# A feed-forward kernel's first product: high and low columns of h side by side, one matmul of 256 columns for two of 128

## The chip, the cores and the metric

The kernel runs on one core of a Trainium2 chip. The metric is device time in microseconds, from one launch. A profiled execution gives the trace: its span runs from the first to the last instruction, and the execution's own time is a little longer.

## The reference, cut to what matters

```python
x = x + gnn(layernorm(x), adj)            # two products with the normalised 2048 x 2048 adjacency
h = layernorm(layernorm(x)) * ln_gamma + ln_beta                   # 2048 tokens, 512 wide
sw1, sw2 = _bit_quant(shared_w1), _bit_quant(shared_w2)            # ternary times a scale per row
shared_out = silu(einsum('btd,fd->btf', h, sw1)) @ sw2.T           # f = 1024
probs = softmax(h @ router_w.T); top_prob, top_idx = max, argmax   # 8 experts
h1 = silu(einsum('btd,efd->ebtf', h, ew1)); eo = einsum('ebtf,edf->ebtd', h1, ew2)
x = x + shared_out + eo of the expert top_idx * top_prob
```

`_bit_quant` gives each row of a weight as -1, 0 or 1 times one scale, the mean of the row's absolute values. All is float32.

## The kernel before, in words

The first 410 us compute x1 (the graph part and its residual), turn the weights into ternary f16 matrices held in SBUF, and write h to memory, each row as a high f16 half and a low f16 half. The change doesn't touch that part, apart from names of PSUM banks.

Then come 39 tiles of 128 tokens: tiles 0 to 15 go through the shared expert, tiles 16 to 38 through one routed expert each, on rows gathered by token. Each has these steps:

- `first_product(n, u)` on TensorE: for 8 blocks `f` of 128 hidden units, 4 blocks `d` of the width and the two halves `h`, a matmul of 128 columns (L1517), all accumulated in float32 in PSUM. Weights are stationary, the columns of h (`ht`, loaded by a transposing DMA) move. High and low half of a block are added into the same 128 columns. The result takes two banks, and two tiles have a pair of banks each (`ps_h`).
- `tile` on VectorE, first part (L1234): for each half of 512 columns, `pre` = PSUM times `s1`, the scale of the weight's row, broadcast along the tokens.
- `tile` on ScalarE: for each half, Silu of `pre` into `h1` (L886) and a copy of `h1` times 16 as f16 (L893, the high half of h1).
- `tile` on VectorE, second part (L1244): for each half, h1 times 16 minus the high half, as f16 (the low half).
- `second_product(n, u)` on TensorE: 16 matmuls of 512 columns (L1545), for 8 blocks and two halves.
- `output` on VectorE (L1272, then L1275 in shared and L1277 in routed tiles): PSUM times the second weight's scale, added to the base row.

`pre` and `h1` are single buffers; h1's halves (`h1hl`) and the second product's banks (`ps_y`) are double. Every engine runs its own queue in order, written out by hand, with semaphores between them. TensorE's is first_product(n + 1), second_product(n), first_product(n + 2), and so on; for shared tiles the router's `logits` of some later tile stand between. VectorE's is, for tile n, the two scaled copies, work passed in as `between`, the two low halves, then output(n - 1), then `route`, the router's small steps. ScalarE's is, for tile n, Silu and high copy twice. In shared tiles two DMA issues stand behind them in ScalarE's queue: `next_base`, and `shared_store(n - 1)`, which waits for output(n - 1):

```python
                tile(n, r % 2, min(n, 2) if isinstance(n, int) else 2)
                if not (isinstance(n, int) and n < 2):
                    next_base(n, r % 2)
                if not (isinstance(n, int) and n == 0):
                    shared_store(n - 1, (r + 1) % 2)
```

Around tile 0 stand the last layer norms (`norm_parts`), a store of x1 (`store_x1`) and, after tile 1, four DMA issues for the column scales (`store_s2`, L849). Ahead of tile 12 ScalarE has an Exp for the router (L924), with a load of its table and one back for Silu; behind tile 12 it issues the store of the gates (`store_gate`, L901). Before routed tiles can be put out, their base rows are gathered on GpSimd's queue, after all shared tiles are stored (`y_stored`), and SyncE loads their scales (`load_scale`).

## Time and profile before

| | us |
|---|---|
| median of 3 runs | 705.63 |
| lowest and highest | 699.36, 707.70 |
| the profiled execution, its own time | 702.86 |
| its span | 701.2 |
| TensorE busy | 648.4 (92%) |
| VectorE busy | 469.2 (67%) |
| ScalarE busy | 389.6 (56%) |
| GpSimd busy | 151.7 (22%) |

Busy time counts instructions that compute; waits and the issuing of DMAs are not in it. The ends of matmuls in the trace are modelled, so the pace of a stream of them is read from start to start.

### The profile page before, as it was taken

Reading aid. Unit: us, or ns where it says so; the run is one execution under the profiler, and the core shown is the slowest. Engines: PE = TensorE matmul, PEld = TensorE weight load, DVE = VectorE, ACT = ScalarE, POOL = GpSimd, SP = SyncE. Lnnn points to the kernel's source line nnn. Section 1 sums busy time; section 2 is a strip of 40 time slices with the busy share of each in tenths; the row PEclk is TensorE's granted clock in tenths of the full one; section 3 lists DMA queues with packets and bytes.
Section 4 is the critical chain, followed back from the end, with each engine's and each line's share of the span. In section 5 each row is a group of like instructions: output and inputs, shape, how many; then the busy total and the mean of one; then the engine's idle time right before and its main releaser. Section 6 shows DMA issues by size and latency. Waiting matters only on the chain.

```text
span 701.2 us, 15954 instructions
## 1 busy us (share of the span) xinstructions
PE 648.4 (92%) x5281; PEld 381.6 (54%) x5281; DVE 469.2 (67%) x1031; ACT 389.6 (56%) x726; POOL 151.7 (22%) x171
## 2 busy tenths in 40 slices
PE   0798999999979999999998789999999999999995
PEld 0343444444434554445434367777767677777773
DVE  4878988566664555688788669756855565555553
ACT  1658648879986776777657653333432242424241
POOL 2234430000000000012323206200021353434322
PEclk9999999999999999999999999999999999999999
DMA  8999962675897777866576896643284876868641
GB/s 348 417 421 417 421 255 62 194 196 155 237 242 251 264 259 253 282 225 237 175 270 218 241 248 166 173 111 96 76 141 131 197 195 176 187 185 181 177 141 31
DMA packets 107103, 151.68 MB, mean 216 GB/s; under 512 B 64286, under 2 KB 64286, under 8 KB 102944
## 3 DMA queue, kind: packets, MB, share of 16 engines
q1 hardware_dynamic: 91280, 117.74, 53.5%
q0 software_dynamic: 6960, 20.99, 9.9%
q10 hardware_dynamic: 8800, 12.09, 5.7%
q8 instruction: 42, 0.69, 0.4%
q14 instruction: 21, 0.17, 0.1%
HBM read 119.57 MB, written 19.16 MB: 198 GB/s over the span
## 4 chain that ended last, share of the span: by engine, by line
PE 54%; DMA 14%; DVE 13%; ACT 9%; issue 7%; SPq 1%; POOL 1%; DVEq 0%; ACTq 0%; POOLq 0%
PE bank L1545 16%; PE bank L1517 16%; PE bank L1390 7%; PE bank L1392 7%; PE bank L1391 7%; DMA region<-in_adj_t 6%; ACT junk L748 4%; DMA work<-in_w 3%; ACT region L760 2%; DVE work L1096 2%; DVE region L986 2%; PE bank L1421 2%; DMA work<-in_adj_t 1%; DVE region L1192 1%; DVE region L982 1%
## 5 line engine op out<-in xcount | busy, mean ns | idle before, releaser
L1545 PE MATMUL bank<-region,work 128*128 (+1 forms) x624 | 141.6, 379 | 4.4 <-DVE work L1244 4.2
L886 ACT ACTIVATE work<-work 128x512 f32<-128x512 f32 x78 | 48.5, 622 | 171.1 <-DVE work L1234 171.1
L1390 PE MATMUL bank<-zreg,work 128*128 (+1 forms) x256 | 98.2, 384 | 12.3 <-DVE work L1164 10.9
L1517 PE MATMUL bank<-zreg,region 128*128 128x128 f16 x1728 | 100.9, 219 | 0.0
L1517 PEld LDWEIGHTS bank<-zreg,region 128*128 (+1 forms) x1728 | 98.1, 98 | 4.2
L1391 PE MATMUL bank<-zreg,work 128*128 (+1 forms) x256 | 98.2, 384 | 0.0
L1392 PE MATMUL bank<-zreg,work 128*128 (+1 forms) x256 | 98.0, 383 | 0.0
L1390 PE MATMUL bank<-region,work 128*128 128x512 f16 x192 | 74.1, 386 | 25.4 <-DVE region L1010 25.4
L1545 PEld LDWEIGHTS bank<-region,work 128*128 128x128 f16 x624 | 58.9, 98 | 70.4 <-issue 7.4
L748 ACT ACTIVATE junk<-work 128x512 f16<-128x512 f32 x124 | 77.6, 625 | 15.9 <-DMA work<-in_w 13.8
L1244 DVE SCALAR_TENSOR_TENSOR work<-work 128x512 f16<-128x512 f32 x78 | 53.7, 691 | 48.8 <-ACT work L893 48.8
L1234 DVE TENSOR_TENSOR work<-bank,s 128x512 f32<-128x512 f32 x78 | 50.2, 685 | 40.6 <-PE bank L1517 39.6
L1391 PE MATMUL bank<-region,work 128*128 128x512 f16 x192 | 74.2, 386 | 0.0
L1392 PE MATMUL bank<-region,work 128*128 128x512 f16 x192 | 74.2, 386 | 0.0
L760 ACT ACTIVATE region<-bank 128x1024 f16<-128x1024 int16 (+1 forms) x58 | 58.2, 1005 | 7.9 <-DVE region L1192 7.1
L1096 DVE TENSOR_SCALAR work<-work,thr 128x512 int16<-128x512 f32 (+1 forms) x96 | 57.7, 631 | 4.3
L804 ACT ACTIVATE work<-work 128x768 f16<-128x768 f32 (+1 forms) x48 | 36.8, 767 | 37.1 <-PE bank L1392 18.8
L591 POOL TENSOR_TENSOR rb<-rb,power 128x2 f32<-128x2 f32 x8 | 8.9, 1118 | 218.9 <-DVE rb L1145 218.9
L893 ACT ACTIVATE work<-work 128x512 f16<-128x512 f32 x78 | 49.1, 629 | 7.1
L1164 DVE SCALAR_TENSOR_TENSOR work<-work 128x768 f16<-128x768 f32 (+1 forms) x48 | 42.3, 884 | 10.4 <-ACT work L804 10.2
L1390 PEld LDWEIGHTS bank<-zreg,work 128*128 128x128 f16 x256 | 25.3, 99 | 41.2 <-DVE work L1164 12.9
L1390 PEld LDWEIGHTS bank<-region,work 128*128 128x128 f16 x192 | 19.1, 99 | 50.4 <-issue 20.7
(154 smaller groups left out, 946.8 us busy)
## 6 DMA issues: line engine op xcount, KB each, us to landing
work<-in_w SPq DMA_DIRECT2D x62, 512.0 KB, 4.1
region<-in_adj SPq DMA_DIRECT2D x16, 1024.0 KB, 10.7
region<-in_adj_t SPq DMA_DIRECT2D x16, 1024.0 KB, 7.5
work<-in_adj_t SPq DMA_DIRECT2D x32, 384.0 KB, 4.4
zreg<-s_scratch SPq DMA_DIRECT2D x24, 256.0 KB, 3.9
xb<-in_w SPq DMA_DIRECT2D x10, 512.0 KB, 4.2
zreg<-in_x SPq DMA_DIRECT2D x4, 1024.0 KB, 9.7
h_scratch<-hb POOLq DMA_DIRECT2D x16, 256.0 KB, 3.4
```

Source lines behind the costliest of these rows:

```text
L748: nc.scalar.activation(junk[:, :], src[:, a * D:(a + 1) * D], ACT.Abs, accum_out=asum[:, b, a:a + 1]).then_inc(abs_ok, 1)
L760: nc.scalar.activation(dst, pst16[turn_bank(q, b)], ACT.Sign).then_inc(wt_ok, 1)
L886: nc.scalar.activation(h1[:, cols], pre[:, cols], ACT.Silu).then_inc(h1_ok, 1)
L893: nc.scalar.activation(h1hl[:, b, 0, cols], h1[:, cols], ACT.Copy, scale=U_SCALE).then_inc(h1hi_ok, 1)
L1096: ins = nc.vector.tensor_scalar(words, rows, thr[:, b, 0, a:a + 1], None, ALU.mult)
L1234: nc.vector.tensor_tensor(pre[:, half * 512:(half + 1) * 512].rearrange("p (f t) -> p f t", f=4), ps_h[b][half][:, :].rearrange("p (f t) - ...
L1244: nc.vector.scalar_tensor_tensor(out=h1hl[:, b, 1, cols], in0=h1[:, cols], scalar=U_SCALE, in1=h1hl[:, b, 0, cols], op0=ALU.mult, op1=ALU. ...
L1390: nc.tensor.matmul(dst, a_hi, b_hi, start=start, stop=False, skip_group_check=True)
L1391: nc.tensor.matmul(dst, a_hi, b_lo, start=False, stop=False, skip_group_check=True)
L1392: return nc.tensor.matmul(dst, a_lo, b_hi, start=False, stop=False, skip_group_check=True)
L1517: last = nc.tensor.matmul(ps_h[b][f // 4][:, (f % 4) * P:(f % 4 + 1) * P], w, ht[n % RING][:, c:c + P], start=(f % 4 == 0 and d == 0 and h ...
L1545: last = nc.tensor.matmul(ps_y[b][:, :].rearrange("p (d c) -> p d c", d=DB), h1hl[:, b, h, f * P:(f + 1) * P], w, start=(f == 0 and h == 0 ...
```

## The change

One matmul of 256 columns takes a weight block over the high and the low columns, which lie side by side in `both` and in PSUM. A tile's first product then has 32 matmuls and fills four banks, 4 to 7, and there is one such buffer. ScalarE copies the low results into `pre` (two copies of 512 columns; the first waits for half of the product, `half_ok`), VectorE adds the high ones to them, and Silu applies the row scale by its per-partition `scale`, which needs an instruction for each of 8 blocks. For routed tiles VectorE first copies the 8 scales of the tile's expert to `s1_now`. The router's results move from banks 6 and 7 to 0 and 1, and the order of the first two tiles on TensorE changes with that.

```diff
--- before.py
+++ after.py
@@ -153,6 +153,7 @@
         thr = sb("thr", [P, 2, 2, 2], F32)
         s1 = sb("s1", [P, 2 * CHUNKS], F32)
         s2 = sb("s2", [P, CHUNKS], F32)
+        s1_now = dinv[:, :].rearrange("p (b f) -> p b f", b=2)
         rt = sb("rt", [P, DB, E], F32)
         r3 = sb("r3", [P, DB, 3, E], BF16)
 
@@ -200,18 +201,20 @@
         before = sb("before", [P, E, E], F32)
         unit = sb("unit", [1, TILES], I32)
 
-        bank = [ctx.enter_context(nc.psum_tensor(f"bank{i}", [P, 512], F32)) for i in range(8)]
-        acc = [bank[i][:, :] for i in range(8)]
-        pst = [bank[6][:, :].bitcast(F16), bank[7][:, :].bitcast(F16)]
-        pst16 = [bank[6][:, :].bitcast(I16), bank[7][:, :].bitcast(I16)]
-
-        ps_h = [[bank[4], bank[5]], [bank[0], bank[1]]]
+        bank = [ctx.enter_context(nc.psum_tensor(f"bank{i}", [P, 512], F32))[:, :] for i in range(4)]
+        banks47 = ctx.enter_context(nc.psum_tensor("banks47", [P, 2048], F32))
+        bank += [banks47[:, i * 512:(i + 1) * 512] for i in range(4)]
+        acc = list(bank)
+        pst = [bank[6].bitcast(F16), bank[7].bitcast(F16)]
+        pst16 = [bank[6].bitcast(I16), bank[7].bitcast(I16)]
+
+        ps_h = banks47[:, :].rearrange("p (f h t) -> p f h t", f=FB, h=2)
         ps_y = [bank[2], bank[3]]
-        ps_r = bank[7]
-        ps_lg = [bank[7], bank[6]]
+        ps_r = bank[0]
+        ps_lg = [bank[0], bank[1]]
         CNT0, LIST0 = 64, 256
-        ps_cnt = bank[7][:, CNT0:CNT0 + (NT + 1) * E].rearrange("p (t e) -> p t e", e=E)
-        ps_list = bank[7][:, LIST0:LIST0 + ROUTED_TILES]
+        ps_cnt = ps_r[:, CNT0:CNT0 + (NT + 1) * E].rearrange("p (t e) -> p t e", e=E)
+        ps_list = ps_r[:, LIST0:LIST0 + ROUTED_TILES]
 
 
         x_in = [sem("x_in0"), sem("x_in1")]
@@ -281,7 +284,10 @@
         base_got = [sem("base_got0"), sem("base_got1")]
         out_stored = [sem("out_stored0"), sem("out_stored1")]
         m1_ok = sem("m1_ok")
+        half_ok = sem("half_ok")
+        pre_lo = sem("pre_lo")
         pre_ok = sem("pre_ok")
+        s1_ok = sem("s1_ok")
         h1_ok = sem("h1_ok")
         h1hi_ok = sem("h1hi_ok")
         h1lo_ok = sem("h1lo_ok")
@@ -876,20 +882,33 @@
             store_x1(2, xg_z)
 
 
-            def tile(n, b, lead):
-
+            def tile(n, b, lead, shared=False):
+
+                for half in range(2):
+                    act.wait_ge(m1_ok if half else half_ok, n + 1)
+                    if lead >= 1:
+                        act.wait_ge(h1_ok, 8 * n - 4 + 4 * half)
+                    quarter = slice(4 * half, 4 * half + 4)
+                    nc.scalar.activation(pre[:, half * 512:half * 512 + 512].rearrange("p (f t) -> p f t", f=4),
+                                         ps_h[:, quarter, 1, :], ACT.Copy).then_inc(pre_lo, 1)
+                scales = s1[:, 0:FB] if shared else s1_now[:, b, :]
+                if not shared:
+                    act.wait_ge(s1_ok, n - NT + 1)
                 for half in range(2):
                     act.wait_ge(pre_ok, 2 * n + half + 1)
                     if lead >= 1:
                         act.wait_ge(h1lo_ok, 2 * n + half - 1)
                     cols = slice(half * 512, half * 512 + 512)
-                    nc.scalar.activation(h1[:, cols], pre[:, cols], ACT.Silu).then_inc(h1_ok, 1)
+                    for f in range(4 * half, 4 * half + 4):
+                        part_cols = slice(f * P, f * P + P)
+                        nc.scalar.activation(h1[:, part_cols], pre[:, part_cols], ACT.Silu,
+                                             scale=scales[:, f:f + 1]).then_inc(h1_ok, 1)
                     if lead >= 2:
                         act.wait_ge(m2_ok, n - 1)
                     if lead == 1:
                         act.wait_ge(ln_normed, 14)
                         act.wait_ge(x1_stored, 16 * NT // 2)
-                    act.wait_ge(h1_ok, 2 * n + half + 1)
+                    act.wait_ge(h1_ok, 8 * n + 4 * half + 4)
                     nc.scalar.activation(h1hl[:, b, 0, cols], h1[:, cols], ACT.Copy, scale=U_SCALE).then_inc(h1hi_ok, 1)
 
             def shared_store(n, b):
@@ -908,7 +927,7 @@
 
             def shared_tile(n, r):
 
-                tile(n, r % 2, min(n, 2) if isinstance(n, int) else 2)
+                tile(n, r % 2, min(n, 2) if isinstance(n, int) else 2, True)
                 if not (isinstance(n, int) and n < 2):
                     next_base(n, r % 2)
                 if not (isinstance(n, int) and n == 0):
@@ -1227,15 +1246,14 @@
 
             def tile(n, b, shared, lead, u, between=()):
 
+                if not shared:
+                    dve.wait_ge(h1_ok, 8 * n - 8)
+                    nc.vector.tensor_copy(s1_now[:, b, :], s1[:, ds(u * FB, FB)]).then_inc(s1_ok, 1)
                 for half in range(2):
-                    dve.wait_ge(m1_ok, n + 1)
-                    if lead >= 1:
-                        dve.wait_ge(h1_ok, 2 * n + half - 1)
-                    nc.vector.tensor_tensor(
-                        pre[:, half * 512:(half + 1) * 512].rearrange("p (f t) -> p f t", f=4),
-                        ps_h[b][half][:, :].rearrange("p (f t) -> p f t", f=4),
-                        s1[:, ds(u * FB + half * 4, 4)].rearrange("p (f a) -> p f a", a=1).to_broadcast([P, 4, P]),
-                        ALU.mult).then_inc(pre_ok, 1)
+                    dve.wait_ge(pre_lo, 2 * n + half + 1)
+                    cols = slice(half * 512, half * 512 + 512)
+                    rows = pre[:, cols].rearrange("p (f t) -> p f t", f=4)
+                    nc.vector.tensor_tensor(rows, ps_h[:, 4 * half:4 * half + 4, 0, :], rows, ALU.add).then_inc(pre_ok, 1)
                 for work_, *args in between:
                     work_(*args)
                 for half in range(2):
@@ -1269,7 +1287,7 @@
                     if lead >= 2:
                         dve.wait_ge(out_stored[b], slot_count(n - NT, b))
                 scale, scaled = (s2bc[:, 1, :], o_t[:, b, :]) if shared else (s2bc[:, b, :], s2bc[:, b, :])
-                chained(nc.vector.scalar_tensor_tensor(out=scaled, in0=ps_y[b][:, :], scalar=1.0 / U_SCALE, in1=scale,
+                chained(nc.vector.scalar_tensor_tensor(out=scaled, in0=ps_y[b], scalar=1.0 / U_SCALE, in1=scale,
                                                        op0=ALU.mult, op1=ALU.mult), y_seq, n + 1)
                 if shared:
                     nc.vector.tensor_tensor(base_t[:, b, 0:D], base_t[:, b, 0:D], scaled, ALU.add).then_inc(y_ok, 1)
@@ -1505,18 +1523,17 @@
 
             def first_product(n, u):
 
-                b = n % 2
                 columns_in(n)
-                if n >= 2:
-                    pe.wait_ge(pre_ok, 2 * n - 2)
+                if n:
+                    pe.wait_ge(pre_ok, 2 * n)
+                both = ht[n % RING].rearrange("p (h d t) -> p d h t", h=2, d=DB)
                 for f in range(FB):
                     for d in range(DB):
                         w = w1t[:, ds(u * (4 * CHUNK) + (f // 2) * CHUNK + d * 2 * P + (f % 2) * P, P)]
-                        for h in range(2):
-                            c = (h * DB + d) * P
-                            last = nc.tensor.matmul(ps_h[b][f // 4][:, (f % 4) * P:(f % 4 + 1) * P], w,
-                                                    ht[n % RING][:, c:c + P], start=(f % 4 == 0 and d == 0 and h == 0),
-                                                    stop=False, skip_group_check=True)
+                        last = nc.tensor.matmul(ps_h[:, f, :, :], w, both[:, d, :, :], start=(f % 2 == 0 and d == 0),
+                                                stop=False, skip_group_check=True)
+                    if f == FB // 2 - 1:
+                        last.then_inc(half_ok, 1)
                 last.then_inc(m1_ok, 1)
 
             def logits(n):
@@ -1542,7 +1559,7 @@
                         nxt = load_unit(ahead)
                     w = w2t[:, ds(u * (4 * CHUNK), 4 * CHUNK)].rearrange("p (d f c) -> p f d c", d=DB, f=FB)[:, f, :, :]
                     for h in range(2):
-                        last = nc.tensor.matmul(ps_y[b][:, :].rearrange("p (d c) -> p d c", d=DB),
+                        last = nc.tensor.matmul(ps_y[b].rearrange("p (d c) -> p d c", d=DB),
                                                 h1hl[:, b, h, f * P:(f + 1) * P], w,
                                                 start=(f == 0 and h == 0), stop=False, skip_group_check=True)
                 last.then_inc(m2_ok, 1)
@@ -1553,14 +1570,13 @@
 
 
             pe.wait_ge(x1_ok, Y_GROUPS[2][0])
-            pe.wait_ge(wt_ok, SHARED_CHUNKS)
+            pe.wait_ge(wt_ok, 2 * CHUNKS)
             first_product(0, 0)
             pe.wait_ge(r3_ok, 1)
-            pe.wait_ge(wt_ok, 2 * CHUNKS)
+            pe.wait_ge(x1_ok, NT - 2)
             logits(0)
-            pe.wait_ge(x1_ok, NT - 2)
+            logits(1)
             first_product(1, 0)
-            logits(1)
             pe.wait_ge(x1_ok, NT)
             second_product(0, 0)
             logits(2)
```

## Rows read from the trace of the kernel before

**Rows 1.** Stretches: each engine's busy us and instructions, clock, DMA share, GB/s.

```profile
424.00:489.00 65.00, 65.00 (x813) 47.99 (x811) 47.08 (x104) 22.76 (x38) 14.11 (x17) 1.00 0.47 130
...
560.00:683.00 123.00, 123.00 (x1381) 88.90 (x1379) 71.24 (x107) 43.36 (x72) 50.73 (x51) 1.00 0.69 178
```

**Rows 2.** Timeline, TensorE, from 566 us: start, us, line, operation, count.

```profile
566.85 3.62 PE L1545 MATMUL bank<-region,work 128*128 x16
570.30 3.74 PE L1517 MATMUL bank<-work,region 128*128 128x128 f16 x64
573.87 3.62 PE L1545 MATMUL bank<-region,work 128*128 x16
```

**Rows 3.** Timeline, VectorE, tile 20.

```profile
560.13 0.75 DVE L1277 SCALAR_TENSOR_TENSOR zreg<-zreg 128x512 f32<-128x512 f32 x1
561.18 1.29 DVE L1234 TENSOR_TENSOR work<-bank,s 128x512 f32<-128x512 f32 x2 [0.29 <-issue]
...
564.61 0.69 DVE L1244 SCALAR_TENSOR_TENSOR work<-work 128x512 f16<-128x512 f32 x1 [0.55 <-ACT work L893]
...
565.94 0.75 DVE L1277 SCALAR_TENSOR_TENSOR zreg<-zreg 128x512 f32<-128x512 f32 x1
```

**Rows 4.** Timeline, ScalarE, tile 20.

```profile
561.99 0.63 ACT L886 ACTIVATE work<-work 128x512 f32<-128x512 f32 x1 [3.21 <-DVE work L1234]
562.71 0.63 ACT L893 ACTIVATE work<-work 128x512 f16<-128x512 f32 x1
563.24 0.61 ACT L886 ACTIVATE work<-work 128x512 f32<-128x512 f32 x1
563.95 0.63 ACT L893 ACTIVATE work<-work 128x512 f16<-128x512 f32 x1
```

**Rows 5.** Groups of ScalarE by shape: busy us, mean ns, then idle.

```profile
L737 ACT ACTIVATE zreg<-bank,dinvz 128x512 f16<-128x512 f32 x16 | 9.8, 689 | 3.1 <-PE bank L1392 3.1
L699 ACT ACTIVATE junk<-zreg,mv 128x512 f16<-128x512 f32 x12 | 8.7, 722 | 1.6 <-DVE mv L961 1.3
...
L924 ACT ACTIVATE zreg<-zreg 128x128 f32<-128x128 f32 x1 | 0.3, 310 | 0.0
```

**Rows 6.** Timeline, VectorE, output in a shared tile.

```profile
447.49 0.69 DVE L1275 TENSOR_TENSOR zreg<-zreg 128x512 f32<-128x512 f32 x1
```

**Rows 7.** Timeline, ScalarE (ACTq: its queue's DMA issues), shared tiles.

```profile
448.35 0.36 ACTq L897 DMA_DIRECT2D base_scratch<-zreg  x1
...
493.40 0.63 ACT L886 ACTIVATE work<-work 128x512 f32<-128x512 f32 x1 [4.64 <-DVE work L1234]
...
498.21 0.36 ACTq L897 DMA_DIRECT2D base_scratch<-zreg  x1
498.74 1.28 ACT L924 ACT_TABLE_LOAD   x1 [2.74 <-DVE zreg L1275]
...
506.58 0.35 ACTq L897 DMA_DIRECT2D base_scratch<-zreg  x1
508.10 0.40 ACTq L901 DMA_DIRECT2D base_scratch<-zreg  x1
...
535.44 0.35 ACTq L897 DMA_DIRECT2D base_scratch<-zreg  x1
```

**Rows 8.** Timeline, ScalarE, DMA issues ahead of tiles 0 and 2.

```profile
414.55 0.38 ACTq L841 DMA_DIRECT2D x_scratch<-work  x1
...
428.40 1.43 ACTq L849 DMA_DIRECT2D s_scratch<-s2t  x4
```

**Rows 9.** Timeline, VectorE, low halves of tile 0, start of tile 1.

```profile
417.89 1.28 DVE L1244 SCALAR_TENSOR_TENSOR work<-work 128x512 f16<-128x512 f32 x2
...
421.83 1.28 DVE L1234 TENSOR_TENSOR work<-bank,s 128x512 f32<-128x512 f32 x2
```

**Rows 10.** Timeline, VectorE, output of tile 17.

```profile
553.18 0.69 DVE L1272 SCALAR_TENSOR_TENSOR zreg<-bank,zreg 128x512 f32<-128x512 f32 x1 [4.78 <-DMA zreg<-s_scratch]
```

**Rows 11.** Timeline, TensorE, the last second product.

```profile
690.79 3.62 PE L1545 MATMUL bank<-region,work 128*128 x16 [0.87 <-DVE work L1244]
```

## The prediction

> **What bounds the kernel now.** I read the stretches table first. From 560 to 683 us, which is routed tiles only, TensorE is busy all of the 123 us, VectorE 71 and ScalarE 43 [rows 1]; the shared tiles of 424 to 489 us look the same. The timeline of TensorE shows what fills it: 64 narrow matmuls of the first product, 3.57 us from their start to the next group's, then 16 wide ones of the second, 3.45 us to the next [rows 2]. A tile costs 7.02 us, and nothing stands between the groups.
>
> So the other two engines have slack, but busy time doesn't say how much, because they hand work to each other and each works its queue in order. I followed tile 20 through both. VectorE starts the scaled copy out of PSUM at 561.18, ScalarE its Silu 0.81 later, then come the high copy (+0.72), the second Silu (+0.53), the second high copy (+0.71), VectorE's second low half (+0.66), the second operation of the output (+1.33), and from that one's start it is 1.05 until VectorE can start the next tile (560.13 to 561.18) [rows 3, 4]. The sum is 0.81 + 0.72 + 0.53 + 0.71 + 0.66 + 1.33 + 1.05 = 5.81 us. It is a ring: VectorE cannot take the next tile's first operation before the output, which stands behind the low halves, which wait for ScalarE. Today the ring takes 5.81 us and TensorE 7.02, so 1.2 us of slack hide it. Whatever the change adds to the ring beyond 1.2 us is paid in every tile.
>
> **The first product.** Columns streamed stay 8192 a tile. A matmul of 128 columns takes 3.57 / 64 = 55.8 ns, of 512 columns 3.45 / 16 = 215.6 ns [rows 2]: a line through both gives 109.1 ns for 256, 3.49 us for 32, and TensorE's tile 6.94. The gain is at most 0.08 x 39 tiles = 3 us, and nothing where TensorE isn't the bound.
>
> The halves now fill banks 4 to 7, so there is one buffer: first_product(n+1) waits for tile n's last add. A second product of 3.45 us lies between, and the add is done about 0.6 (copy) + 0.7 (add) + 0.6 us of queueing and handing over after the first product ends. This wait costs nothing, except in tile 1, where a longer term covers it.
>
> **Silu.** Two instructions of 512 columns become eight of 128 with a per-partition scale. The trace has no such one. Nearest are an Exp of 128 columns, 0.31 us, and a 512-column one with a per-partition operand, 0.72 against 0.63 without [rows 4, 5]. So one takes 0.31 + 0.09 = 0.40 us. Successive independent ones overlap by 0.10 (the high copy from 562.71 runs to 563.34, the Silu behind it starts at 563.24 [rows 4]), so they start 0.31 apart. Four and the handing over to the high copy: 3 x 0.31 + 0.40 + 0.09 = 1.42 us, where it is 0.72 and 0.71 now. That adds 1.41 us to the ring. Bounds: below, if the operand cost nothing and 0.22 lay between starts, 3 x 0.22 + 0.31 + 0.09 = 1.06, 0.7 a tile less; above, no overlap at all, 3 x 0.40 + 0.40 + 0.09 = 1.69, 0.54 more. I take the middle, as both rows measure their part.
>
> The Trainium skill (ScalarE: Activation LUTs, What ACT_TABLE_LOAD costs) gives 186 ns + 0.833 ns per element, 93 ns for each pointer operand and 93 ns overlap. By these figures the starts are 0.29 apart and four take 1.36 us; the sum below would be about 5 us less. The Trainium skill (VectorE: DVE Perf Modes, The TRN2 errata) speaks against the edit: a fixed latency is paid for each instruction, so many small tiles pay it again and again. The trace agrees: an eighth of a tile costs 0.31 us and half a tile 0.63.
>
> **The ring of the routed tiles.** VectorE's add takes the place of its multiply (same elements, one PSUM source; VectorE's operations of this size take 0.69 to 0.75 [rows 3], I take 0.69). ScalarE's two copies of the low halves come before it in another idle time: the first waits for half of the first product, done long before VectorE is through with the output. The copy of the scale and its two waits add some 0.2 us in front of the add (0 to 0.4). The ring is 5.81 + 1.41 + 0.20 = 7.42, and 7.45 with something for the loop's branch. It exceeds TensorE's 6.94, so it becomes the bound, by 0.43 us over today's 7.02.
>
> **The ring of the shared tiles** is worse. There ScalarE's queue has, behind each tile's high copies, the store of the tile before, which waits for VectorE's output. Today what follows the store is a Silu with time to spare. After the change the first low copy of the next tile stands there, and VectorE can't add without it. Within a tile, from the first Silu: 1.42 + 0.53 + 1.42 + 0.66 = 4.03 to the second low half, 1.33 + 0.69 to the end of the output [rows 3, 6]: 6.05. The store is issued 0.17 later (448.18 to 448.35), takes 0.36, and the next ScalarE instruction comes 0.17 behind it (498.57 to 498.74): 0.70 [rows 6, 7]. The copy from PSUM, by the one that has a per-partition operand, takes 0.69 - 0.09 = 0.60 [rows 5], handing over 0.03, the add to the Silu 0.81. Period: 6.05 + 0.70 + 0.60 + 0.03 + 0.81 = 8.19 us, against 7.02 now and the logits' short matmuls. Bounds without those of the Silus: 8.0, if the issue hides 0.2, to 8.4.
>
> **The sum**, as times of each tile's first Silu.
> Tile 0: the x1 store goes out at 414.55 [rows 8] and takes 0.38, the copy follows at 415.10, first Silu 416.54. Waiting for all transposes before tile 0's first product costs nothing: it still ends before that copy's turn. Tile 0's low halves end at 421.26, and 2.66 us of layer-norm work stand ahead of the next tile, as now (419.17 to 421.83 [rows 9]): tile 1 at 424.73. Then the output, the store, four DMA issues of the column scales (1.43 [rows 8]) and the copy, all in a row now: tile 2 at 434.40. Tile 3, 0.4 late through layer-norm work ahead of the low halves: 442.99. Eight periods of 8.19: tile 11 at 508.5. It is at 493.40 now [rows 7]: +15.1.
> Tile 12: 6.05 + 0.70, table load 1.28 and Exp 0.31 [rows 5, 7], two copies 1.0, table load for Silu and handing over 1.3 = 10.65. Tile 13: the store of the gate goes out 1.52 after the tile's own, takes 0.40 [rows 7], and stands ahead of the copy: 6.05 + 0.17 + 1.52 + 0.40 + 0.17 + 1.44 = 9.75. Tiles 14 to 16, three periods: 24.6. Tile 16 at 553.5.
> From the end of tile 15's output to that of tile 17 runs a chain of DMAs (store, gathers, transposes, scales): 535.27 to 553.18, 17.9 us [rows 7, 10]. VectorE stalled 4.8 us for it, most of it inside its slack. After the change it ends at 559.55 + 17.9 = 577.5, where the two tiles would be ready at 573.8. The stall is 3.7, all of it on the path. Tile 19 at 580.7, tile 20 at 588.1, against 561.99 [rows 4]: +26.1, so +11.0 between tiles 11 and 20.
> Eighteen routed periods, 134.1, and 4.8 from the last first Silu to the last second product: 138.9. It was 690.79 - 561.99 = 128.8 [rows 4, 11]: +10.1. What follows is unchanged.
> Total +15.1 + 11.0 + 10.1 = +36.2 us on the profiled execution's 702.86: **739 us**. That execution is 0.4% below the median 705.63, so the ratio to the median is 1.047.
>
> **The rivals.**
> A. TensorE stays the bound, and the kernel ends faster than before: the narrow Silus and copies fit into slack, 0.08 us is won in each tile, the bigger matmuls pay: 702.86 - 3 = 700. It decides if both rings stay under 6.94, that is, 0.5 us less than I have in the routed and 1.25 in the shared tiles. For it: ScalarE is busy only 43 of 123 us. Against it: the ring, which can be read off. 7%.
> Its stronger form is that the weight loads of the narrow matmuls, not their columns, set their pace. With half the loads the first product would then come down to the second's pace for a column, 8192 x 215.6 / 512 = 3.45 us, 4.7 us in all: 698. The two rows speak against it, 0.436 ns a column in the one and 0.421 in the other [rows 2]. 1%. The Trainium skill (TensorE: Matmul & The Clock Gate, Back-to-back issue gap) has such a rule, about 81 ns for a matmul of 128 columns in a stream with weight loads and 131 for 512; the trace's 55.8 and 215.6 agree with neither.
> B. Four narrow Silus cost about as much as one wide one (0.81 with its scale). The rings are then some 6.2 and 7.0, only the start, tiles 12 and 13 and the longer end cost something: about 710. For it: they are independent and queued. Against it: the 0.31 us of the Exp, which is mostly fixed cost. 9%.
> C. They don't overlap, as each reads a per-partition operand: 0.54 x 38 tiles more, 760. For it: no row has two such back to back that weren't held up otherwise. 12%.
> My forecast, both rings bound, has the rest, 70%.
>
> **Range and chances.** The bounds of the copy of the scale, the DMA issue and the Silus' spacing move the forecast by 0.5 us a tile either way, 19 us: 720 to 758. With C it holds 8 in 10: 720 to 760. Within 2% of 705.6 (about what a measurement of this kernel can tell from no change) are A and B, up to 719.7: 0.16; faster by over 2% (below 691.5) is none of the cases: 0.01; slower 0.83.
>
> **What the profile after would show.** TensorE idle before the second product in nearly all tiles, released by VectorE's low half (L1244 now); its share down from 92% to about 88%. Silus of 0.40 us starting 0.31 apart. First Silus 8.2 us apart in shared tiles and 7.45 in routed ones. VectorE idle before its add in shared tiles, released by ScalarE's low copy, which starts 0.7 us behind the output's end. The first product 3.49 us. Wrong would be: no idle time ahead of the second product (A), Silus closer than 0.2 (B) or 0.4 apart (C), or a low copy that starts ahead of the store's wait, which would bring the shared tiles down to the routed ones' pace.

## The result and the profile after

| us | before | after |
|---|---|---|
| median of 4 executions (lowest to highest), same chip | 703.68 (699.36 to 707.7) | 728.12 (727.63 to 728.99) |
| ratio, 95% interval | | 1.0358 (1.032 to 1.0396) |
| the profiled execution | 702.86 | 728.99 |
| its span | 701.2 | 727.4 |

The change makes the kernel 24 us slower. The prediction was 739, with 720 to 760 as its range. It started from a median of 705.63; a fourth execution of the kernel before, 701.74, lowers that to 703.68. The first part of the page after:

```profile
PE 659.1 (91%) x4033; PEld 364.4 (50%) x4033; DVE 473.3 (65%) x1054; ACT 483.6 (66%) x1038; POOL 155.4 (21%) x171
```

ScalarE works 94 us more (483.6 for 389.6), and no engine has over 91% of the span. As in the prediction, the busy shares don't say who sets the time. The stretches table after has the same columns as [rows 1]:

```profile
424.00:489.00 65.00, 58.35 (x464) 39.17 (x463) 41.06 (x91) 36.22 (x92) 14.79 (x17) 1.00 0.44 117
...
560.00:683.00 123.00, 119.79 (x798) 77.20 (x796) 69.24 (x116) 80.31 (x200) 54.56 (x52) 0.99 0.73 176
```

TensorE, busy without a break in both stretches before, now idles 6.65 us of 65 in the shared tiles, and 3.2 of 123 in the routed ones.

Where the 26.2 us of span came from can be read off the timeline of ScalarE, by the start of each tile's first high copy (L893 before, L912 after):

| first high copy of tile | 0 | 3 | 11 | 12 | 13 | 19 | 20 | 38 | end of span |
|---|---|---|---|---|---|---|---|---|---|
| before | 415.81 | 438.35 | 494.12 | 502.63 | 510.18 | 556.90 | 562.71 | 688.05 | 701.2 |
| after | 416.20 | 442.94 | 507.75 | 518.22 | 527.57 | 578.48 | 585.49 | 713.54 | 727.4 |
| later by | 0.4 | 4.6 | 13.6 | 15.6 | 17.4 | 21.6 | 22.8 | 25.5 | 26.2 |

Half is gone by tile 11: shared tiles 3 to 11 are 8.10 us apart where they were 6.97 (two short gaps of a tile catching up among them; at even pace, from tile 6 on, they were 7.1 to 7.2 apart). Tiles 12 to 20 add 9.2 more. The 18 routed periods from tile 20 to 38 are 7.11 apart where they were 6.96, 2.7 us in all.

The timeline of ScalarE after, first in a shared and then in a routed tile:

```profile
455.86 0.36 ACTq L916 DMA_DIRECT2D base_scratch<-zreg  x1
456.41 1.08 ACT L892 ACTIVATE work<-banks 128x512 f32<-128x512 f32 x2 [2.77 <-DVE zreg L1293]
457.84 1.28 ACT L904 ACTIVATE work<-work,s 128x128 f32<-128x128 f32 x4 [0.35 <-DVE work L1256]
459.15 0.63 ACT L912 ACTIVATE work<-work 128x512 f16<-128x512 f32 x1
...
598.48 1.28 ACT L904 ACTIVATE work<-work,dinv 128x128 f32<-128x128 f32 x4 [0.50 <-DVE work L1256]
599.78 0.63 ACT L912 ACTIVATE work<-work 128x512 f16<-128x512 f32 x1
600.32 1.26 ACT L904 ACTIVATE work<-work,dinv 128x128 f32<-128x128 f32 x4
...
602.65 0.60 ACT L892 ACTIVATE work<-banks 128x512 f32<-128x512 f32 x1 [0.41 <-PE banks L1533]
```

The shared tile shows the longer ring that the prediction describes: ScalarE idles 2.77 us because the store's issue waits for VectorE's output, and the low copies stand behind it. In the routed tile no store is in the way. Compare with [rows 4]: a Silu's start to its high copy's was 0.72 us and is 1.30. VectorE's timeline after, from the end of that shared ring and from two routed tiles:

```profile
455.00 0.69 DVE L1293 TENSOR_TENSOR zreg<-zreg 128x512 f32<-128x512 f32 x1
...
457.04 1.29 DVE L1256 TENSOR_TENSOR work<-banks,work 128x512 f32<-128x512 f32 x2 [0.79 <-ACT work L892]
...
596.60 0.75 DVE L1295 SCALAR_TENSOR_TENSOR zreg<-zreg 128x512 f32<-128x512 f32 x1
597.55 0.17 DVE L1251 COPY dinv<-s 128x8 f32 x1 [0.19 <-issue]
597.67 1.29 DVE L1256 TENSOR_TENSOR work<-banks,work 128x512 f32<-128x512 f32 x2
600.45 0.69 DVE L1262 SCALAR_TENSOR_TENSOR work<-work 128x512 f16<-128x512 f32 x1 [1.49 <-ACT work L912]
602.28 0.69 DVE L1262 SCALAR_TENSOR_TENSOR work<-work 128x512 f16<-128x512 f32 x1 [1.14 <-ACT work L912]
...
603.61 0.75 DVE L1295 SCALAR_TENSOR_TENSOR zreg<-zreg 128x512 f32<-128x512 f32 x1
604.84 0.17 DVE L1251 COPY dinv<-s 128x8 f32 x1 [0.48 <-issue]
```

From the output's last operation to the next tile's copy of the scales it is 0.95 us in the one tile (596.60 to 597.55) and 1.23 in the next (603.61 to 604.84). The second one crosses the end of the loop's body, which holds two tiles. So routed tiles alternate between 7.01 and 7.28 us, and the mean of the two, 7.145, is what the ring costs.

TensorE's timeline after, behind the stall of tile 19 and later in the routed tiles:

```profile
577.91 5.54 PE L1533 MATMUL banks<-zreg,region 128*128 128x256 f16 x32 [2.71 <-DVE work L1256]
583.28 3.62 PE L1562 MATMUL bank<-region,work 128*128 x16
...
593.68 3.66 PE L1533 MATMUL banks<-work,region 128*128 128x256 f16 x32
597.17 3.62 PE L1562 MATMUL bank<-region,work 128*128 x16
600.63 3.66 PE L1533 MATMUL banks<-work,region 128*128 128x256 f16 x32
...
635.61 3.86 PE L1533 MATMUL banks<-work,region 128*128 128x256 f16 x32
639.42 3.71 PE L1562 MATMUL bank<-region,work 128*128 x16
```

From 593.68 to 600.63 a tile costs TensorE 6.95 us, 3.49 for the first product and 3.46 for the second. There it is behind the ring and catching up at 0.2 us a tile. By 635.61 it has caught up: the first product then takes 3.81 us (to 639.42), and no idle time stands before either group. The program has no wait inside a first product. What has become late is TensorE's queue, which hands the matmuls to the engine: it passes the wait ahead of this product (L1528) at 634.85, just behind VectorE's second add (it ends at 634.81), only 0.76 us before the first matmul. For every weight block the queue forms an address in a register (`FUSED_REGOPS`), most of them 124 ns apart:

```profile
L1533 PEldq FUSED_REGOPS  x31: 46/46/46, 635.1 to 639.1; - x31
```

The first 22 matmuls start 109 ns apart; then the queue's lead is used up and the others start 124 ns apart, once 182. A group whose queue is late looks busy in this view, so the distance from start to start must be read, not the idle column.

### The profile page after: what moved, and what is told of

The parts are those of the page before. It is cut to its first block, busy times and chain, and to the rows that moved or that the text cites. A ratio compares the mean times of both kernels' runs of the same rounds, so it can differ in the third digit from the quotient of the medians.

```text
span 727.4 us, 13812 instructions
## 1 busy us (share of the span) xinstructions
PE 659.1 (91%) x4033; PEld 364.4 (50%) x4033; DVE 473.3 (65%) x1054; ACT 483.6 (66%) x1038; POOL 155.4 (21%) x171
## 4 chain that ended last, share of the span: by engine, by line
PE 42%; DVE 16%; ACT 14%; DMA 13%; issue 9%; ACTq 2%; SPq 1%; POOL 1%; DVEq 0%; POOLq 0%
PE banks L1533 10%; PE bank L1562 9%; DMA region<-in_adj_t 6%; ACT work L904 6%; PE bank L1408 5%; PE bank L1410 5%; PE bank L1409 5%; DMA work<-in_w 5%; ACT junk L754 3%; PE banks L1410 2%; PE banks L1409 2%; PE banks L1408 2%; DVE region L1005 2%; DVE zreg L1290 2%; DVE work L1115 2%
## 5 line engine op out<-in xcount | busy, mean ns | idle before, releaser
L1262 DVE SCALAR_TENSOR_TENSOR work<-work 128x512 f16<-128x512 f32 x78 | 54.0, 693 | 93.0 <-ACT work L912 92.9
L1533 PE MATMUL banks<-zreg,region 128*128 128x256 f16 x864 | 104.1, 279 | 10.4 <-DVE work L1256 9.1
L1533 PEld LDWEIGHTS banks<-zreg,region 128*128 (+1 forms) x864 | 85.2, 99 | 29.5 <-issue 11.4
L892 ACT ACTIVATE work<-banks 128x512 f32<-128x512 f32 x78 | 44.7, 592 | 72.5 <-DVE zreg L1293 34.9
L754 ACT ACTIVATE junk<-work 128x512 f16<-128x512 f32 x124 | 77.6, 626 | 17.4 <-DMA work<-in_w 15.1
L1408 PE MATMUL bank<-zreg,work 128*128 128x512 f16 (+1 forms) x192 | 73.8, 384 | 11.5 <-DVE work L1183 10.5
L904 ACT ACTIVATE work<-work,dinv 128x128 f32<-128x128 f32 x184 | 58.4, 388 | 28.3 <-DVE work L1256 27.5
L1410 PE MATMUL bank<-zreg,work 128*128 128x512 f16 (+1 forms) x192 | 73.5, 383 | 0.0
L1409 PE MATMUL bank<-zreg,work 128*128 128x512 f16 (+1 forms) x192 | 73.5, 383 | 0.0
L1408 PE MATMUL bank<-region,work 128*128 128x512 f16 x112 | 43.7, 390 | 25.4 <-DVE region L1029 25.4
L766 ACT ACTIVATE region<-banks 128x1024 f16<-128x1024 int16 (+1 forms) x58 | 58.2, 1006 | 8.2 <-DVE region L1211 6.8
L1256 DVE TENSOR_TENSOR work<-banks,work 128x512 f32<-128x512 f32 x78 | 50.5, 686 | 15.3 <-ACT work L892 15.3
L912 ACT ACTIVATE work<-work 128x512 f16<-128x512 f32 x78 | 49.1, 630 | 3.5
L1533 PE MATMUL banks<-work,region 128*128 128x256 f16 x384 | 45.1, 274 | 2.4 <-DVE work L1256 2.4
L904 ACT ACTIVATE work<-work,s 128x128 f32<-128x128 f32 x128 | 40.6, 388 | 6.7 <-DVE work L1256 6.6
L1409 PE MATMUL bank<-region,work 128*128 128x512 f16 x112 | 43.9, 392 | 0.0
```

The lines of the kernel that those rows point to most:

```text
L754: nc.scalar.activation(junk[:, :], src[:, a * D:(a + 1) * D], ACT.Abs, accum_out=asum[:, b, a:a + 1]).then_inc(abs_ok, 1)
L766: nc.scalar.activation(dst, pst16[turn_bank(q, b)], ACT.Sign).then_inc(wt_ok, 1)
L904: nc.scalar.activation(h1[:, part_cols], pre[:, part_cols], ACT.Silu, scale=scales[:, f:f + 1]).then_inc(h1_ok, 1)
L912: nc.scalar.activation(h1hl[:, b, 0, cols], h1[:, cols], ACT.Copy, scale=U_SCALE).then_inc(h1hi_ok, 1)
L1256: nc.vector.tensor_tensor(rows, ps_h[:, 4 * half:4 * half + 4, 0, :], rows, ALU.add).then_inc(pre_ok, 1)
L1262: nc.vector.scalar_tensor_tensor(out=h1hl[:, b, 1, cols], in0=h1[:, cols], scalar=U_SCALE, in1=h1hl[:, b, 0, cols], op0=ALU.mult, op1=ALU. ...
```

## The experiments

A ratio is to the kernel before on the same chip. "Pace" is the distance between first high copies of successive tiles.

**e1: the store behind the next tile's low copies.** In the kernel after, shared_store(n - 1) is issued between the low copies and the first Silu of tile n + 1, no longer ahead of the copies (the gate's store moves with it; the base load stays).

```diff
+            for issue, *args in late:
+                issue(*args)
...
-                if not (isinstance(n, int) and n == 0):
-                    shared_store(n - 1, (r + 1) % 2)
+                late = [(shared_store, n - 2, r % 2)]
```

> The changed kernel with the shared tiles' stores (and the gate's) issued by ScalarE behind the next tile's two low copies instead of ahead of them. My theory (a ring of VectorE and ScalarE, in which the store's wait and issue delay the low copy): first Silus of shared tiles come 7.2 us apart instead of 8.1, as TensorE with its logits then binds; tiles 3 to 11 give back 7.4 us, tiles 13 to 17 some 3 more; total 728.1 - 11 = 717. The routed tiles stay at 7.14. Rival, that the narrow Silus alone make ScalarE's chain too long: the pace stays near 8.1 and the total at 726 to 728.

Measured: 716.25 us (715.7 to 719.93), ratio 1.0228 (1.0189 to 1.0267), span 713.9. ScalarE's timeline in shared tiles:

```profile
455.66 0.60 ACT L892 ACTIVATE work<-banks 128x512 f32<-128x512 f32 x1 [0.41 <-PE banks L1533]
456.58 0.36 ACTq L918 DMA_DIRECT2D base_scratch<-zreg  x1
457.74 1.28 ACT L906 ACTIVATE work<-work,s 128x128 f32<-128x128 f32 x4 [1.49 <-DVE work L1256]
```

The low copies now wait for TensorE and not for VectorE's output, and the store lies in idle time. Tile 3 to 11 takes 58.88 us where it took 64.81, a pace of 7.36 for 8.10 (7.2 was expected); routed tiles stay at 7.01 and 7.28. The position of one DMA issue in ScalarE's queue is worth 9 us by the ratios (1.0358 less 1.0228, of 703), and 11.4 by the spans from tile 0 on (13.4 less the 2.0 by which tile 0 was earlier): some 40% of the loss. This confirms the second ring of the prediction.

**e2: one Silu of 512 columns for four of 128.** In the kernel after, with the row's scale left out, so the scale is not applied. All else, copies and single buffer included, stays.

```diff
-                    for f in range(4 * half, 4 * half + 4):
-                        part_cols = slice(f * P, f * P + P)
-                        nc.scalar.activation(h1[:, part_cols], pre[:, part_cols], ACT.Silu,
-                                             scale=scales[:, f:f + 1]).then_inc(h1_ok, 1)
+                    nc.scalar.activation(h1[:, cols], pre[:, cols], ACT.Silu).then_inc(h1_ok, 4)
```

> The changed kernel with one Silu of 512 columns per half, without the per-row scale (the scale of the first weight is left out of the result). My theory: the chain from Silu to high copy falls from 1.31 to 0.72 us, twice in a ring. Routed ring 7.14 - 1.18 = 5.96, shared 8.10 - 1.18 = 6.92, both under TensorE's 6.95 and 7.15: total 708 to 711, the rest over 703.7 being start, tiles 12 and 13 and the end. Rival, that the single buffer in PSUM or the low copies hold TensorE up: over 720.

Measured: 707.17, ratio 1.0075 (1.0053 to 1.0098), span 703.3. That is just under the expected 708 to 711. Routed tiles run at 6.95 us, TensorE's own pace. Shared tiles 3 to 11 are 6.90 apart: there VectorE and ScalarE catch up with TensorE, whose own groups are 7.15 apart (466.09 to 473.24). So the many short Silus are necessary for nearly all of the loss: without them about 5 us of 25 remain (by the ratios), and these lie ahead of tile 3 (26.17 us from tile 0 to tile 3, against 22.54 before and 26.74 after) and at tile 12 (9.78 against 8.51).

**e3: TensorE's part alone.** The 32 matmuls of 256 columns and the single buffer, in the kernel before; VectorE scales the high half as before, and the low half's sum is never read, so it is left out of the result.

```diff
+                        last = nc.tensor.matmul(ps_h[:, f, :, :], w, both[:, d, :, :], start=(f % 2 == 0 and d == 0),
+                                                stop=False, skip_group_check=True)
...
-                        ps_h[b][half][:, :].rearrange("p (f t) -> p f t", f=4),
+                        ps_h[:, 4 * half:4 * half + 4, 0, :],
```

> TensorE's part alone: 32 matmuls of 256 columns into the one buffer of four banks, but the other engines work as before the change (VectorE scales the high half, one Silu per half); the low half of h is computed and left out. My theory: TensorE binds, first product 3.49 us, 0.08 us less in each of 39 tiles, 703.7 - 3 = 700.5; the single buffer costs nothing. Rival, that the wait for the one buffer costs: first products start late, over 706.

Measured: 703.55 over 10 runs (701.95 to 706.68), ratio 1.0012 (0.9987 to 1.0037), span 700.5. The 3 us did not show. TensorE's gain is there where TensorE is the bound: routed tiles are 6.95 us apart, not 7.02, and tile 21 to 38 takes 117.96 us for 119.24. It is given back in two places, first at tile 12 (gap 9.77 for 8.51). ScalarE's and TensorE's timelines there:

```profile
498.96 0.31 ACT L930 ACTIVATE zreg<-zreg 128x128 f32<-128x128 f32 x1
500.87 1.28 ACT L892 ACT_TABLE_LOAD   x1 [1.60 <-issue]
```

```profile
502.40 3.66 PE L1521 MATMUL banks<-zreg,region 128*128 128x256 f16 x32
507.89 1.17 PE L1597 MATMUL bank<-zreg 128*128 128x23 f16 x16 [1.84 <-DVE zreg L1352]
```

Here Silu's table is loaded 1.60 us after the Exp ends; in the kernel before it begins at once (Exp at 500.03, load at 500.36). TensorE then idles 1.84 us. The other place is behind tile 19's stall, where tile 20 to 21 takes 7.14 us for 6.10; with two buffers TensorE could have a first product ready ahead, with one it can't, which is argued and not shown. The load of the table begins 0.07 us behind the end of VectorE's first multiply for tile 12 (500.11 + 0.69 = 500.80), for which that Silu waits; in the kernel before it begins ahead of the multiply (501.18). So here it stands behind the Silu's wait, and its 1.28 us lie on the path. e2 has the same (add ends at 503.72, load at 503.79), which is part of its loss at tile 12. What puts the load behind the wait was not tried.

**e4: eight Silus of 128 columns in the kernel before**, with a per-partition scale of one, VectorE's multiply and both buffers kept. It leaves nothing out.

```diff
-                    nc.scalar.activation(h1[:, cols], pre[:, cols], ACT.Silu).then_inc(h1_ok, 1)
+                    for f in range(4 * half, 4 * half + 4):
+                        part_cols = slice(f * P, f * P + P)
+                        nc.scalar.activation(h1[:, part_cols], pre[:, part_cols], ACT.Silu,
+                                             scale=before[:, 1, 0:1]).then_inc(h1_ok, 1)
```

> The kernel before with eight Silus of 128 columns and a per-partition scale of one; everything else as before. My theory: the ring grows from 5.81 by 1.18 to 6.99 us, and by another 0.28 over a loop's back edge, so 7.13 on average in routed tiles against TensorE's 7.02: 2 us there, 1 in the start, 1 at tile 12, 0.6 at the end, total 708. Rival, that ScalarE's added work is hidden wherever TensorE binds: 704 or less. Rival, that narrow Silus alone explain most of the change's loss: over 716.

Measured: 721.88 (716.95 to 724.46), ratio 1.0295 (1.0267 to 1.0324), span 715.3. It missed: the Silus alone bring most of the loss, some 20 us, where 708 was expected. Routed tiles alternate between 6.97 and 7.26, as worked out. But shared tiles 3 to 11 run at 7.41, because there the router's small steps on VectorE stand in the ring, which the expectation left out: 0.85 us to the next multiply (463.83 to 464.68), and 1.16 in every second tile, across the end of the loop's body (471.22 to 472.38). The ring of the shared tiles is then 5.81 + 1.16 (for the Silus), with 0.61 + 0.85 from output to multiply in place of the 1.05 of routed tiles, that is 7.38, and 7.69 in every second tile; gaps of 7.39 and 7.70 were measured. And 12 to 14 and 18 to 19 stall (gaps of 9.76, 8.85, 9.66, and 8.34, 11.45, for 8.51, 7.55, 7.15, and 7.10, 11.10 before). TensorE's timeline at tile 12:

```profile
512.69 1.17 PE L1597 MATMUL bank<-zreg 128*128 128x23 f16 x16 [4.97 <-DVE zreg L1350]
513.70 6.13 PE L1549 MATMUL bank<-region,work 128*128 128x512 f16 x16
519.67 3.74 PE L1521 MATMUL bank<-zreg,region 128*128 128x128 f16 x64
```

TensorE waits 4.97 us for the router's list, and the second product behind it takes 5.97 us to the next group instead of 3.46; the stretches table gives a granted clock of 0.66 there:

```profile
510.00:520.00 10.00, 7.31 (x38) 3.53 (x39) 6.51 (x16) 3.70 (x10) 3.26 (x3) 0.66 0.52 77
```

The profiled execution was the shortest of six. Two had 716.95 and 718.32 us at a mean granted clock of 0.987, four had 721.6 to 724.5 at 0.978 to 0.982. The longer ones go with a lower clock; in which stretch they lost it no trace shows. The trace, of the shortest one, shows 15 us of the 20: from tile 0's first high copy to the end it takes 300.6 us, 285.4 in the kernel before.

**e5: VectorE's output one tile later.** In the kernel after, output(n - 2) stands behind the add of tile n, where VectorE waits for the Silus anyway; the stores move one tile later with it.

```diff
                     nc.vector.tensor_tensor(rows, ps_h[:, 4 * half:4 * half + 4, 0, :], rows, ALU.add).then_inc(pre_ok, 1)
+                if not (isinstance(n, int) and n < 2):
+                    m = n - 2
+                    output(m, b, own, 2 if not isinstance(n, int) else min(m - (0 if own else NT), 2))
...
-                    output(n - 1, (r + 1) % 2, True, min(n - 1, 2) if isinstance(n, int) else 2)
```

> The changed kernel with VectorE's output of tile n - 2 between the adds and the low halves of tile n, where VectorE waits for the Silus, instead of the output of tile n - 1 behind the low halves; ScalarE's store and base load move with it (behind tile n, with nothing to wait for). My theory: the output's 2.0 us leave the ring, and in shared tiles the store's wait too. The ring falls to about 5.1 us, TensorE binds everywhere: routed 6.95, shared 7.15, total 700 to 703, about the time of the kernel before or a little under. Rival, that the engines' added work as such (ScalarE busy 484 us, PSUM read by two engines while TensorE writes it) slows the kernel: over 715, as the work is all still there.

Measured: 708.26, ratio 1.0075 (1.0056 to 1.0093), span 705.1, against 1.0358 for the change as it stands. The edit takes the output's two operations, some 1.4 us, out of the ring, and in shared tiles the store's wait as well. The two together give back 20 of 25 us; how they share it this run doesn't tell. Shared tiles are 7.15 apart (6 to 11), routed ones 6.95 from tile 21 on, TensorE's own pace. It misses the expected 700 to 703 by some 5 us, and 3.5 of them lie between tiles 11 and 21 (78.20 us, 74.69 in the kernel before), where VectorE waits for transfers. The waits of this kernel from 420 us on:

```profile
ACT work L892 <- PE banks L1530: 75.4, 68, 3.5
...
DVE zreg L1298 <- DMA zreg<-x_scratch: 6.2, 3, 3.1
DVE zreg L1298 <- DMA zreg<-s_scratch: 5.8, 1, 5.8
```

In the kernel after, `ACT work L892 <- DVE zreg L1293` had 34.9 us and `DVE work L1262 <- ACT work L912` 92.9. Both rings are broken. VectorE waits 12 us for these loads, where the kernel before has one wait of 4.8 for the scales, and the gaps are 9.45 us at tile 16 and 10.11 at tile 20. That the later outputs made the loads later is argued, not shown.

**e6: the same shift in the kernel before**, as the counterpart of e5.

```diff
                         ALU.mult).then_inc(pre_ok, 1)
+                if not (isinstance(n, int) and n < 2):
+                    m = n - 2
...
+                    output(m, b, own, 2 if not isinstance(n, int) else min(m - (0 if own else NT), 2))
```

> The same move of the output made in the kernel before. My theory: its ring (5.81 us) is under TensorE's 7.02 already, so only the stalls at the start, at tile 12 and around tile 19 can change, within 2 us either way: 700 to 704. Rival, that the order itself is worth something in either kernel: under 698.

Measured: 707.63, ratio 1.0072 (1.0045 to 1.0099), span 705.3. It missed, and not in the transfers alone: routed tiles 26 to 34 alternate between 7.15 and 7.24 to 7.30, though the ring is wide open. TensorE's timeline:

```profile
631.87 1.03 PE L1542 MATMUL bank<-region,work 128*128 x4
633.10 2.76 PE L1542 MATMUL bank<-region,work 128*128 x12 [0.20 <-issue]
635.70 3.74 PE L1514 MATMUL bank<-zreg,region 128*128 128x128 f16 x64
```

The second product stops after its fourth matmul for 0.20 us, put down to TensorE itself. It is where TensorE's queue reads the number of a later tile's expert from SBUF (`load_unit`). Here are these reads from 560 to 690 us (shortest, median and longest in ns), in the kernel before and in e6:

```profile
L1552 PEldq TENSOR_LOAD <-unit x18: 297/302/311, 559.9 to 679.1; - x18
...
L1549 PEldq TENSOR_LOAD <-unit x18: 297/480/910, 560.3 to 681.8; - x18
```

The read at this stop lasts 0.84 us (631.82 to 632.66), and the matmuls go on at 633.10. So the queue, late by a long read, holds TensorE up. All kernels that moved the output have such reads (e5 a median of 0.51 us, e10 0.47), the others hardly any; in e5 the queue has lead enough and the pace stays 6.95. What makes the reads long is open. e5 and e6 together say that the shift is no gain by itself; it pays only where the ring is the bound.

**e7 and e8: one more add of 512 columns on VectorE ahead of each routed tile's output**, in the kernel after (e7) and before (e8). Its result is not used.

```diff
+                if not shared:
+                    nc.vector.tensor_tensor(junk[:, :], gb[:, 0, :], gb[:, 1, :], ALU.add)
```

> The changed kernel with one more VectorE operation of 512 columns (0.61 us from start to start, result unused) ahead of the output in routed tiles. My theory: routed tiles are bound by the ring (7.14 us), so each grows by 0.61 to 7.75: 18 x 0.61 = 11 us from tile 20 to 38, 12 in all, 740. Rival, that TensorE or ScalarE binds the routed tiles: under 732.

> The same extra operation in the kernel before. My theory: its ring goes from 5.81 to 6.42 us, under TensorE's 7.02, so it costs nothing but a part at the stall of tile 19 and 0.6 at the end: 702 to 704. Rival, that VectorE's work shows in the time wherever it is: 714.

Measured: e7 740.66, ratio 1.0524 (1.049 to 1.0558), span 739.7; e8 704.6, ratio 1.0025 (0.9995 to 1.0055), span 702.9, so 0.6 us over what was expected and far from the rival's 714. The added work in e7's timeline of VectorE:

```profile
648.57 0.69 DVE L1290 TENSOR_TENSOR junk<-gb 128x512 f16<-128x512 f32 x1
649.17 0.69 DVE L1292 SCALAR_TENSOR_TENSOR zreg<-bank,zreg 128x512 f32<-128x512 f32 x1
```

The add puts the next operation 0.60 us later (648.57 to 649.17), and routed tiles go from 7.01 and 7.28 to 7.60 and 7.88: the whole 0.6, in every tile. In the kernel before the same add leaves the pace at 7.02 and 7.03; it only slows the catching up behind tile 19's stall (6.4 to 6.7 us for 5 tiles, where it was 5.81 and 6.10 for 2). So the ring is the bound after and not before, though VectorE is busy for 56% of the routed stretch in the one kernel and 58% in the other (69.24 and 71.24 of 123 us).

**e9: e4 with the list's matmuls behind the second product of tile 12**, so that this product doesn't stand behind TensorE's wait for the list (the list's matmuls, L1598, are in the lines left out).

```diff
+            second_product(ROUTE_TILE, 0)
...
-            second_product(ROUTE_TILE, 0)
```

> The kernel before with narrow Silus, as in the run with them alone (721.9 us, where I had expected 708), and TensorE's 16 matmuls that list the tokens placed behind the second product of tile 12 instead of ahead of it. There TensorE had stood idle for 5.0 us ahead of them, and the second product behind took 6.0 us instead of 3.45, at a granted clock of 0.66 in those 10 us. My theory: the miss is this stall with the clock's fall behind it; tile 14's first Silu comes 7.2 to 7.6 us after tile 13's instead of 9.7, total 719 or less. Rival, that the list isn't what holds tile 14 up: no change, 722.

Measured: 721.99, ratio 1.0258 (1.0224 to 1.0292), span 718.8, where e4 had 1.0295 (1.0267 to 1.0324). TensorE's timeline:

```profile
513.20 3.63 PE L1549 MATMUL bank<-region,work 128*128 128x512 f16 x16 [2.61 <-DVE work L1248]
516.67 1.11 PE L1598 MATMUL bank<-zreg 128*128 128x23 f16 x16
```

It missed the expected 719 or less. Locally the stall shrank: TensorE idles 2.61 us for 4.97, the second product takes 3.47 for 5.97, and tile 14's gap falls from 9.66 to 8.17 (7.2 to 7.6 expected). The stall at the transfers ahead of the routed tiles only moved: tile 18's gap grew from 8.34 to 11.89 and tile 19's fell from 11.45 to 7.59. From tile 0 to tile 20 it takes 157.3 us, 1.5 less than e4, and from there to tile 38 130.0, 2.0 more, with gaps of 7.55 and 8.12 at tiles 31 and 35 where TensorE stops inside a first product; why is open. The intervals overlap, so no gain is shown.

**e10: e5 with its transfers put right**: both last stores ahead of tile 17, the last shared output straight behind tile 16, `between` work ahead of the output, and the gates' store two tiles later.

```diff
             shared_store(NT - 2, 0)
-            tile(NT + 1, 1, 2)
             shared_store(NT - 1, 1)
+            tile(NT + 1, 1, 2)
...
             for n in range(NT, NT + 5):
                 tile(n, n % 2, False, 2, load_unit(n))
+                if n == NT:
+                    output(NT - 1, 1, True, 2)
```

> The changed kernel with the output moved into the wait for the Silus (which was 708.3 us, bound by TensorE at 6.95 us a tile but with 5 us of waits for DMAs around tiles 16 and 20), and three things put back or aside: the list of tokens is read out ahead of the output again, tile 15 is put out at the end of tile 16, and the gates are stored two tiles later. My theory: the two waits shrink by 2 to 4 us, total 704 to 706; with all waits gone it could reach 702. Rival, that the waits come from elsewhere in the DMA queues: 707 to 709 as before.

Measured: 719.32, ratio 1.0199 (1.0178 to 1.022), span 716.6. It missed both the expected 704 to 706 and the rival's 707 to 709, and is 11 us slower than e5. ScalarE's timeline, first at the last stores, then in a routed tile:

```profile
539.62 4.16 ACTq L916 DMA_DIRECT2D base_scratch<-zreg  x2
543.88 1.08 ACT L892 ACTIVATE work<-banks 128x512 f32<-128x512 f32 x2 [5.50 <-DVE zreg L1301]
...
640.34 0.58 ACT L892 ACTIVATE work<-banks 128x512 f32<-128x512 f32 x1
643.46 0.60 ACT L892 ACTIVATE work<-banks 128x512 f32<-128x512 f32 x1 [2.54 <-PE banks L1532]
```

The last store waits in ScalarE's queue for an output that is itself late, and tile 17's low copies stand behind it: a gap of 10.79 us, what e1 had removed is back at this place. That part is read off the trace. From tile 18 to 34 the tiles are mostly 7.2 to 8.2 apart, with ScalarE's second low copy waiting for TensorE, and only from 35 on near 6.95, where e5 has 6.95 from 21 on with the same loop. In nine of these tiles the first product takes 4.05 to 4.39 us to the next group; in the one from 668.17 on nearly all its matmuls are 124 ns apart or more. The queue has no lead there, as in the kernel after at 635.61, and its reads of the expert's number are long (up to 0.94 us). Why it loses its lead here and not in e5 is open. No kernel tried was faster than the one before.

## Why the prediction was right, and what was off

Its mechanism held: two rings between ScalarE and VectorE take TensorE's place as the bound, and the share of busy time hid it. e7 and e8 show the routed ring as the bound after and not before. e1 takes the store out of the shared ring and e2 the short Silus out of both; e5 takes out the output, and with it the store. What each gives back (9, 20 and 20 of 25 us) can't be added up, as each brings the rings below or near TensorE's pace. The forecast of the added span was 36.2 us and 26.2 were measured, so it was too high by more than a third; the range of 40 us held that. Its chances add up to 99 in 100, as the rest behind A, B and C is 71 and not 70. On the way from 737.4 us (701.2 + 36.2) to the measured span of 727.4, by first high copies (the prediction's first Silus plus its 1.42):

| stretch | predicted | measured | off |
|---|---|---|---|
| tile 0 starts | 417.96 | 416.20 | -1.8 |
| tile 0 to 11 | 91.96 | 91.55 | -0.4 |
| tile 11 to 20 | 79.6 | 77.74 | -1.9 |
| tile 20 to the last second product | 137.48 | 131.43 | -6.1 |
| to the end | 10.4 | 10.4 | 0.0 |

- **The shared ring** was right: 8.19 us predicted, 8.10 measured. From the output's start to the low copy it took 1.41 us (455.00 to 456.41), predicted 0.69 + 0.70.
- **Tiles 12 and 13** were 10.47 and 9.35 for 10.65 and 9.75. The chain of DMAs took 18.2 us (556.26 to 574.46) for 17.9, the stall 4.15 for 3.7.
- **The routed ring** is the term that was mis-sized, 7.45 us against a measured 7.145, and 7.11 as the mean of the 18 periods, as the last two, behind the loop, are only 6.92 and 6.79: 18 x 0.34 = 6.1 us of the 10. Of the 0.3, 0.24 are the Silus: a group takes 1.30 to its high copy, predicted 1.42. One Silu takes 0.388 (0.40 predicted) and they start (1.28 - 0.388) / 3 = 0.297 apart (0.31), and the handing over is 0.02 (1.28 to 1.30), where 0.09 was put down. The other 0.07 is two errors that partly cancel. Output to add was taken as 1.05 + 0.20 (copy of the scales) + 0.03 (loop) = 1.28, and is 1.07 or 1.35, a mean of 1.21: the copy adds 0.02 and not 0.20, the loop's end 0.28 in every second tile, 0.14 in the mean and not 0.03.
- The Trainium skill (ScalarE: Activation LUTs, What ACT_TABLE_LOAD costs) gives 186 + 0.833 x 128 + 93 = 386 ns for one and 93 less, 293 ns, from start to start. The trace's 388 and 297 agree; its figures were closer here than my rows from other shapes.
- **The start** was 1.8 us earlier than forecast: the first Silu, predicted for 416.54, came at 414.90. The store of x1 was issued at 412.80 and not at 414.55, just behind VectorE's x1 (L1211, ready at 412.77), and the first low copy followed it at 413.23. I see no part of the change in it: tile 0's first high copy comes anywhere from 413.90 (e7) to 417.59 (e9).
- **TensorE.** 3.49 us for the first product was exact. Its tile of 6.95 is reached in e2, e3 and e5. But the gain of 3 us that the prediction put at "at most" did not show at all in e3. Its signature was wrong too: TensorE's share was to fall to 88% and is 91%, and idle time ahead of nearly all second products is there only in shared tiles (0.27 us, with 0.24 and 0.48 ahead of first products). In routed tiles the ring holds up TensorE's queue, and the first product is stretched.
- **The rivals.** A (TensorE stays the bound) and its stronger form fall with the 7.145 of the ring and the 3.49. B (four narrow Silus cost as much as one wide one) falls with 1.30 for 0.72; C (no overlap) with 0.297 us between starts, less than the 0.388 of one.
- What it didn't have: losses in one stretch change those of the next, as the kernel catches up or a stall moves. e4 alone costs 20 us, where its routed pace of 7.12 explains 0.1 us a tile; e2 alone costs 5; their sum is about the whole. How the Silus' 20 us in e4 divide between router steps, the list and the transfers is only partly shown, as e9 shortened one stall and lost the gain again later.

## What to carry to other kernels

Before adding work to an engine that is "only half busy", follow one tile through all engines and add up the ring of hand-overs: slack is the bound's period less the ring's, 1.2 us here and 0.9 in every second tile, at the loop's end, and not the idle share. A DMA issue that waits in a compute engine's queue is part of the ring of everything behind it; moving one store behind two copies was worth some 10 us. Splitting one instruction into four cost 0.58 us each time (1.30 for 0.72) though all four overlapped.

## What the runs showed of the hardware

- The granted clock fell behind stalls. In the kernel after, the first product behind 2.71 us of idle time took 5.37 us to the next group (577.91 to 583.28) and not 3.49, and another behind 2.22 us has 5.32 us (516.84), where 3.66 is usual. The stretches table after:

```profile
510.00:520.00 10.00, 7.54 (x42) 4.36 (x41) 7.79 (x21) 7.12 (x15) 0.00 (x0) 0.89 0.16 55
520.00:530.00 10.00, 8.29 (x49) 4.58 (x47) 6.19 (x14) 5.35 (x14) 1.93 (x2) 0.77 0.34 56
...
580.00:590.00 10.00, 10.00 (x66) 6.93 (x65) 6.23 (x10) 6.31 (x15) 3.73 (x4) 0.87 0.65 177
```

  It is 1.00 in these stretches before. A clock between the levels of 1.2 and 2.4 GHz in a stretch is a mix of both. In e9, 2.61 us of idle time were followed by a second product at full speed (3.47 us), so the length of one idle time doesn't decide it. Behind tile 19 it cost nothing that can be seen, as tile 20 came 7.01 us later, at the ring's own pace.
- A matmul of 256 columns takes 3.49 / 32 = 109 ns in a stream with a weight load each, on the line through the 55.8 and 215.6 ns of [rows 2]. The Trainium skill (TensorE: Matmul & The Clock Gate, Back-to-back issue gap) has 81 ns for 128 and 131 ns for 512 columns in such a stream; no run here came to those.
- TensorE's queue forms a register address for each weight block in 124 ns or more (the kernel after, from 635.1 us), longer than the 109 ns of a matmul of 256 columns. It costs nothing while the queue is ahead; without a lead a first product takes 3.81 us (after) to 4.39 (e10) and not 3.49.
- The end of a loop's body costs VectorE 0.28 us, every second tile (1.23 less 0.95), and all of it counts once the ring is the bound.
